# Input statistics ahead of a gating multiply, thresholds scaled on another engine, prologue and last tile in another order: one attention and expert layer on one core

## The reference

```
x = x + attention(layernorm(x))            # 16 heads of 8, one shared key and value head, causal
x = x + experts(layernorm(x))
  xn = rmsnorm(x) * gamma;  q = xn @ wq.T  # 2 halves x 8 heads x 64
  sim = q . keys                           # 2 x 8 lists of 32 per row
  best 16 of the sums sx[i] + sy[j] per head; softmax over them
  h = gelu(xn . table_down[e]) * prob;  out = sum h * table_up[e]
```

## Time and profile before

| | |
|---|---|
| median of 3 runs | 849.4 us (849.34 to 853.87) |
| the profiled execution | 852.14 us, of which the span from first to last instruction is 850.3 us |
| mean granted TensorE clock | 0.968 of full speed |
| busy, share of the span | PE 83%, PEld 58%, DVE 88%, ACT 80%, POOL 77% |
| one iteration of the loop | 47.70 us |

### The profile page before, as it was taken

How to read it: one execution, slowest core, us unless ns; L and a number is a source line. 1 busy time by engine, 2 the same in 40 slices (tenths; PEclk the granted TensorE clock), 3 DMA queues, 4 the chain that set the end, 5 groups by cost and what they waited for, 6 DMA issues and landing times.

```text
span 850.3 us, 21025 instructions
## 1 busy us (share of the span) xinstructions
PE 703.9 (83%) x6148; PEld 492.1 (58%) x6214; DVE 750.8 (88%) x2934; ACT 676.8 (80%) x927; POOL 658.2 (77%) x370
## 2 busy tenths in 40 slices
PE   3886878897979888897979888897979888887867
PEld 2652536574646656574646666574646666564746
DVE  4419599999999999999999999999999999898984
ACT  1365688989888898989888898888888898868471
POOL 2111488897979799898979799898979798887761
PEclk9897989999999999999999999999999999899988
DMA  6322121120303121120302021120302121000000
GB/s 176 57 40 56 21 55 28 29 57 10 74 2 67 19 60 26 31 55 10 74 2 67 19 60 26 35 51 10 76 0 67 19 55 27 13 21 1 20 6 7
DMA packets 34736, 32.53 MB, mean 38 GB/s; under 512 B 5520, under 2 KB 32784, under 8 KB 32976
## 3 DMA queue, kind: packets, MB, share of 16 engines
q1 hardware_dynamic: 34608, 32.12, 17.3%
q10 hardware_dynamic: 96, 0.02, 0.0%
HBM read 19.93 MB, written 5.24 MB: 30 GB/s over the span
## 4 chain that ended last, share of the span: by engine, by line
PE 47%; DVE 25%; issue 14%; ACT 9%; DMA 2%; POOL 1%; SPq 1%; DVEq 1%; ACTq 0%; POOLq 0%
DVE prob L1061 12%; PE misc L1305 6%; PE misc L1465 6%; PE score L1342 5%; PE score L1394 5%; PE score L1285 5%; PE score L1255 4%; ACT prob L750 3%; PE score L1287 3%; PE misc L1307 3%; ACT late_scores L616 2%; PE score L1258 2%; DVE halves L901 2%; DVE late_scores L907 2%; PE score L1406 2%
## 5 line engine op out<-in xcount | busy, mean ns | idle before, releaser
L516 POOL TENSOR_TENSOR acc<-acc,prob 128x1024 f32<-128x1024 f32 x184 | 435.5, 2367 | 16.2 <-POOL acc L516 0.6
L1061 DVE SCALAR_TENSOR_TENSOR prob<-score,cut,prob 128x1024 f32<-128x1024 f32 x256 | 314.5, 1277 | 22.8 <-ACT prob L750 21.4
L750 ACT ACTIVATE prob<-score,neg_lse 128x1024 f32<-128x1024 f32 x256 | 279.0, 1119 | 36.8 <-PE score L1394 30.0
L1394 PE MATMUL score<-sel_unit,pieces_t 128*128 128x512 bf16 x479 | 148.2, 395 | 72.5 <-DVE prob L1061 47.5
L643 ACT ACTIVATE probs<-score 128x512 f32<-128x512 f32 x192 | 110.2, 597 | 27.4 <-PE score L1287 23.3
L516 POOL TENSOR_TENSOR acc<-prob 128x1024 f32<-128x1024 f32 x32 | 75.6, 2361 | 64.5 <-DVE prob L1061 64.5
L1394 PEld LDWEIGHTS score<-sel_unit,pieces_t 128*128 128x128 f16 x512 | 40.1, 101 | 118.6 <-DVE prob L1061 83.4
L1342 PEld LDWEIGHTS score<-xn_kept,wdt 128*128 128x128 f32 x480 | 72.4, 191 | 29.4 <-issue 6.4
L1342 PE MATMUL score<-xn_kept,wdt 128*128 128x128 f32 x480 | 85.0, 278 | 3.8 <-DVE prob L1061 3.4
L1255 PE MATMUL score<-k_ahead,q_ahead 128*128 128x256 bf16 (+1 forms) x512 | 70.3, 246 | 12.6 <-ACT probs L643 7.0
L1465 PEld LDWEIGHTS misc<-wu,gated_t 128*128 128x128 f32 x480 | 66.0, 199 | 9.8 <-issue 1.7
(11 more groups left out here) (151 smaller groups left out, 1437.6 us busy)
## 6 DMA issues: line engine op xcount, KB each, us to landing
q_scratch<-qk_piece SPq DMA_DIRECT2D x16, 192.0 KB, 2.1
q_ahead<-q_scratch SPq DMA_DIRECT2D x16, 192.0 KB
q_stack<-q_scratch SPq DMA_DIRECT2D x16, 192.0 KB
xin<-x SPq DMA_DIRECT2D x16, 128.0 KB, 3.0
q_ahead<-q_scratch SPq DMA_DIRECT2D x16, 128.0 KB
q_stack<-q_scratch SPq DMA_DIRECT2D x16, 128.0 KB
xres<-x SPq DMA_DIRECT2D x16, 128.0 KB, 3.4
x_kept<-x SPq DMA_DIRECT2D x16, 128.0 KB, 2.0
```

The source lines that it names most:

```text
L516: eng.tensor_tensor(acc[:, j, :], so_far, prob[:, j * FH + h, :], ALU.add).then_inc(acc_added, FH - h if last else 1)
L750: eng.activation(prob[:, g, :], score[g % BUFS][:, :], ACT.Exp, bias=neg_lse[:, j, h:h + 1]).then_inc(prob_made, 1)
L1061: eng.scalar_tensor_tensor(prob[:, g, :], score[g % BUFS][:, :], cut[:, j, h:h + 1], prob[:, g, :], ALU.is_ge, ALU.mult).then_inc(prob_mas ...
L1394: ins = eng.matmul(score[g % BUFS][:, cols], pieces_t[:, j, h, :], sel_unit[:, cols], start=True, stop=True)
```

## The change

1. VectorE does `ln1(i+3)` straight after `make_y`, ahead of `gate(i-1, 0)`; it stood behind `norm_x2`.
2. `scale_cut` moves from VectorE to ScalarE, behind `xn_back`, and writes a new tensor `limit` that the masks read.
3. Prologue: the DMAs of the two expert tables (`wdt`, `wu`) go from before the first `store_pieces` to behind `stack_pieces(0)`, with a semaphore of their own. ScalarE does `xn_back(0)` ahead of `qk_middle_piece(2)`. TensorE waits for the last maxima copy of batch 1 and runs `keep_busy` twice, five matmuls each, around `xn_transpose(0)`.
4. Iteration 0: `weigh_values` and `invert_sums` come ahead of the first score maxima of batch 2.
5. Iteration 15: ScalarE does `pieces_back` ahead of `best_exp`. TensorE adds only head 2, after all pair scores; VectorE adds heads 3 to 7 with four additions.

```diff
 prologue, SyncE
-                                 (keyt[:, :], keys), (wdt[:, :], down),
-                                 (wu[:, :, :], up.rearrange("(c p) d -> p c d", p=P))):
+                                 (keyt[:, :], keys)):
                     eng.dma_start(dst, src).then_inc(weights_in, 16)
...
                 stack_pieces(0)
+                eng.dma_start(wdt[:, :], down).then_inc(tables_in, 16)
+                eng.dma_start(wu[:, :, :], up.rearrange("(c p) d -> p c d", p=P)).then_inc(tables_in, 16)
 ScalarE
+            def scale_cut(b):
+                eng.wait_ge(cut_made, every(cut_made, b))
+                if not later(b):
+                    eng.wait_ge(unit_step, 9)
+                eng.activation(limit[:, :, :], cut[:, :, :], ACT.Copy, scale=unit[:, :]).then_inc(cut_scaled, 1)
...
+                xn_back(0)
                 qk_middle_piece(2)
-                xn_back(0)
...
-                if m:
+                if m and d:
                     max_scores_back(i + 2, 0)
                 if a:
                     invert_sums(i + 1)
+                if m and not d:
+                    max_scores_back(i + 2, 0)
...
+                if f and not a:
+                    pieces_back(i, 0)
+                    pieces_back(i, 1)
                 if f:
                     best_exp(i)
...
+                if f and a:
                     pieces_back(i, 0)
                     pieces_back(i, 1)
...
                     xn_back(i + 1)
                 if f:
+                    scale_cut(i)
                     pair_probs(i, 0, 1)
 VectorE
-                eng.scalar_tensor_tensor(prob[:, g, :], score[g % BUFS][:, :], cut[:, j, h:h + 1], prob[:, g, :],
+                eng.scalar_tensor_tensor(prob[:, g, :], score[g % BUFS][:, :], limit[:, j, h:h + 1], prob[:, g, :],
...
-                eng.tensor_tensor(prob[:, 2 * FH - 2, :], ...)
-                eng.tensor_tensor(prob[:, 2 * FH - 3, :], ...)
+                for n in range(4):
+                    g = 2 * FH - 2 - n
+                    if n > 0:
+                        eng.wait_ge(late_added, n)
+                    eng.tensor_tensor(prob[:, g, :], prob[:, g, :], prob[:, g + 1, :], ALU.add).then_inc(late_added, 1)
...
                     make_y(i + 1)
+                if p:
+                    ln1(i + 3)
                 if d and f:
                     gate(i - 1, 0)
                 if f:
                     shift_best(i)
                 if a:
                     norm_x2(i + 1)
-                if p:
-                    ln1(i + 3)
...
-                if f:
-                    scale_cut(i)
 TensorE
-                eng.wait_ge(weights_in, 6 * 16)
+                eng.wait_ge(weights_in, 4 * 16)
...
                 project_qkv(2, x2_made, 0)
+                eng.wait_ge(max_kept, every(max_kept, 1))
+                keep_busy(score[1], 5)
                 xn_transpose(0, v_next_made, every(v_next_made, 2))
+                keep_busy(score[1], 5)
...
-                if m:
+                if m and d:
                     scores_for_max(i + 2, 0)
                 if a:
                     weigh_values(i + 1, 0, max_t_made, i + 1)
                     weigh_values(i + 1, 1, max_t_made, i + 1)
+                if m and not d:
+                    scores_for_max(i + 2, 0)
...
                     for h in range(4, FH):
                         pair_scores(i, 1, h, a, m)
-                        if not a and h < 7:
-                            sum_last_tile(h - 2)
...
                 if f and not a:
+                    sum_last_tile(2)
                     finish_last()
```

More of the change, by code:

```diff
@@ L162, in build @@
         cut = sb("cut", [P, TILES, FH])
+        limit = sb("limit", [P, TILES, FH])
         shifted = sb("shifted", [P, TILES, FH, TOPK])
@@ L185, in build @@
         weights_in = signal("weights_in")
+        tables_in = signal("tables_in")
         wa_in = signal("wa_in")
@@ L267, in build @@
         acc_added = signal("acc_added", TILES * (FH - 1))
-        late_added = signal("late_added", 2)
+        late_added = signal("late_added", 4)
         last_hidden = signal("last_hidden", 2)
@@ L1034, in place_cut @@
                                          ALU.mult, ALU.add).then_inc(cut_made, 1)
[L1036 to L1041, removed]
             def sum_best(b):
@@ L1066, in add_late_heads @@
                 eng.wait_ge(prob_masked, at(prob_masked, LAST, TILES * FH))
[L1067 to L1070, removed]
-                                  ALU.add).then_inc(late_added, 1)
+                for n in range(4):
[3 more added lines that the diff above has]
+                    eng.tensor_tensor(prob[:, g, :], prob[:, g, :], prob[:, g + 1, :], ALU.add).then_inc(late_added, 1)
             def gate_last(j):
@@ L1119, in prologue @@
                 eng.tensor_tensor(wkey_sq[:, :], wkey[:, :], wkey[:, :], ALU.mult).then_inc(unit_step, 1)
-                eng.wait_ge(weights_in, 6 * 16)
+                eng.wait_ge(tables_in, 2 * 16)
                 eng.tensor_scalar(wdt[:, :], wdt[:, :], gam[:, 0:1], None, ALU.mult).then_inc(setup_done, 1)
@@ L1445, in finish_last @@
                 sum_transposed(misc, acc[:, 1, :], False, False)
-                eng.wait_ge(late_added, 2)
-                sum_transposed(misc, prob[:, 2 * FH - 3, :], False, True, acc_tp)
+                eng.wait_ge(late_added, 4)
+                sum_transposed(misc, prob[:, 2 * FH - 5, :], False, True, acc_tp)
                 eng.wait_ge(x2_copied, every(x2_copied, LAST))
```

## The result

| | before | after |
|---|---|---|
| median (6 runs each) | 850.81 us (849.34 to 853.87) | 857.25 us (853.43 to 860.35) |
| profiled execution | 852.14 us, span 850.3 | 856.89 us, span 855.1 |
| mean granted TensorE clock | 0.968 | 0.964 |

The change makes the kernel slower by a little, but clear of the scatter: ratio 1.0065, 95% interval 1.0036 to 1.0095. The forecast was 843.6 us, range 836 to 853. In what follows medians are over all runs of a kernel, but the ratio of e2 leaves out its two slowest (865.5 and 866.1 us), which are in the slow state.

What follows compares the result with a forecast made beforehand. Two nearly equal loops bound it: VectorE's own list, and masks through TensorE and ScalarE back to VectorE. Terms +2.0 +0.4 -2.6 -0.5 -0.9 -3.8 -0.4 = -5.8 us gave 846.3 profiled, 843.6 median, range 836 to 853.

Steps and rivals of the forecast that it cites:

- so ln1 costs 0.96 us: Loop: moved ahead of the gate, ln1 fills the 0.55 us wait, delays the gate 0.41, of which 0.24 is absorbed.
- Late xn: Loop: beside VectorE's folds GpSimd's xn pair takes about 3.5 us instead of 1.58; 0 per iteration at full clock.
- Clock drops in the loop: Loop: TensorE's longer pause lowers its clock in 2 of 12 iterations, +1.0 us each, +2 in all (0 to +12).
- Rival 1: Loop: the clock falls in every iteration, +12 us instead of +2: 853.6 us, or 856 with second drops; chance 0.18.
- scale_cut: Move to ScalarE: nothing in iterations 0 to 13, +0.4 us in iteration 14, where the first mask must wait for ScalarE.
- Tables: Prologue: with the table DMAs moved, the first write of queries lands earlier, -2.6 us (bounds 0 and -2.6).
- keep_busy: Prologue: added matmuls let the key scores run at full clock, -0.5 us (bounds 0 and -1.7).
- Order of iteration 0: Weighted values start 1.8 us earlier, the copy of the maxima moves onto the path: -0.9 us (bounds 0 and -1.8).
- Iteration 0 itself: Iteration 0: ln1 stands where VectorE waits, so 0.
- Last tile: Iteration 15: masks end 5.0 us earlier, four additions replace two: -3.8 us (+2.5 to -5); pieces_back ahead of best_exp -0.4.
- Rival 3: Last tile or prologue gives nothing, as with additions and a half-clock sum ending the chain: 846 to 848 us; chance 0.14.

Runs made afterwards that it cites:

- e2: Kernel before with only the move of ln1 ahead of the gate: 860.66 us, ratio to before 1.0069.
- e13: Kernel after with ln1's last step made by two one-column operations instead of one of two columns, same place: 848.93 us, ratio to before 0.9959.
- e5: e3 with VectorE also waiting in the loop for both xn operations ahead of the first fold: 861.5 us, ratio to before 1.0096.
- e3: Kernel after with only ln1's last step, the addition of epsilon, moved back behind norm_x2: 848.37 us, ratio to before 0.9944.
- e4: Kernel after with scale_cut back on VectorE: 856.24 us, ratio to before 1.0042.
- e12: e9 with scale_cut back on VectorE between the folds: 843.65 us, ratio to before 0.9892.
- e1: Kernel after with ln1 back behind norm_x2, everything else of the change kept: 846.83 us, ratio to before 0.993.
- e8: e1 without the prologue's ten small matmuls and with xn copied behind the middle piece again: 845.42 us, ratio to before 0.9918.
- e9: e8 and e6 joined: ln1 back, no small prologue matmuls or earlier xn copy, heads 2 and 3 on TensorE: 844.61 us, ratio to before 0.9908.
- e10: e9 with the order of iteration 0 as in the kernel before: 843.1 us, ratio to before 0.990.
- e7: e1 with 20 small unread matmuls ahead of TensorE's last-tile wait for the four additions: 844.77 us, ratio to before 0.9905.
- e6: e1 with TensorE adding heads 2 and 3 of the last tile, VectorE making three additions: 845.13 us, ratio to before 0.9911.

## Why the prediction was wrong

The step that failed is "so ln1 costs 0.96 us", carried to the new place. The duration was read where ln1 stood before; ahead of the gate its last step is held behind GpSimd's piece of sim for 0.85 us in nearly every iteration. In the kernel before it is 18.18 us from the last mask to the next statistics; with the forecast's terms that becomes 18.18 + 0.41 - 0.24 = 18.35. e13, where the step isn't held, has 18.38; the kernel after has 19.03.

With e13 the loop takes 713.33 - 140.90 = 572.43 us. That is +0.2 against before, with 47.56 at full clock and 48.48 in two drops, where the forecast had 47.70, 48.7 and two drops. With the held step it is +7.7, and the first held step lies in the stretch of iteration 0. Over both stretches the kernel after takes 8.6 us more than e13 (630.19 against 621.60), out of the 10.6 us that forecast and measured sum lie apart. The forecast and the measured median lie 13.65 apart. Of the 3 us more, 1.4 are in the level of before (849.4 from three runs, 850.81 from six), and the rest in where the two profiled executions lie among their runs.

The sign stood in the trace of the kernel before: its `bounded` step, 128x2 too, took 0.41 us beside GpSimd's pieces in the loop and 0.17 alone, and one `ln_tmp` of the prologue 1.14.

Point by point:

- **Late xn**: right. 3.34 us (forecast 3.5), made by the folds (e5), and at full clock it takes back what the earlier fold gave (e3, e13). The forecast had read the contention in one direction only: VectorE's folds hold up GpSimd. What decided the case was a VectorE step held up by GpSimd.
- **Clock drops in the loop**: about right in this trace, three instead of two, 1.0 to 1.1 us each, and partly by luck: with the held step e2 has five and e4 six. Rival 1 named a time (853.6 to 856) close to what came, by a mechanism that did not occur: nine of twelve iterations had no drop.
- **scale_cut**: right in the loop (e12). In iteration 14 the first mask starts 5.59 us after the x2 statistics instead of 5.07: +0.5, forecast +0.4.
- **Tables**: right, 2.5 us over all traces (forecast 2.6), 1.98 in the profiled pair. In that one TensorE's new last wait is for `k_ahead` on ScalarE's queue.
- **keep_busy**: wrong in sign. The key scores did speed up, 3.42 to 1.96 us; what came earlier by it ran into the folds of batch 1. Forecast -0.5, measured +0.8 to +1.5 (e13 against e12, e1 against e8).
- **Order of iteration 0**: right, -1.0 where the clock is low in the same places (forecast -0.9); the pair e9 and e10 alone would give -1.8.
- **Iteration 0 itself** was put at 0 and took 1.33 more. 0.87 of it is the first held step of ln1, which comes ahead of the statistics that end this stretch. The rest comes before the eighth mask (19.52 instead of 19.02 us after the statistics): there too xn is late (6.08 us, before 5.58) and the clock down.
- **Last tile**: the masks were about right. The last of them ends 69.3 us after the x2 statistics of iteration 14 instead of 74.8, -5.5, where the forecast's terms for this part make -5.0. The end was mis-sized: 17.4 us from there on instead of 13.0, so +4.5, where the forecast had +1.2. The four additions took 5.71 us (forecast 5.4), the last sum 3.78 (forecast 2.0), since TensorE had waited 2.80 us and came back at half clock, and the first output matmuls 3.11 instead of 1.95 for the same reason. Rival 3 had named this. e7 shows the clock's part, and e6 that an even split between the engines avoids it.
- **Iteration 13**: -1.57 was not forecast. Its wait of 1.46 us ahead of mask 3 in the kernel before is gone after, together with the clock drop of the earlier trace rows; where the drop comes again (e9) the iteration takes 47.54 us, where not (e1) 46.76. That part is scatter of the clock.

## What to carry to other kernels

An instruction's duration belongs to its place. Least, median and most of a small step over one trace show whether it is sometimes held. Before moving one, list what the other engine that shares its SBUF ports runs at the new place, and ask both ways who holds up whom, for steps of 128x2 too. If a small step is caught, changing its form can be cheaper than moving it. Work that gets faster upstream (the key scores) or an engine that gets all of a shared task (the four additions) should be followed to what it now lies beside and who now waits.

## What the hardware showed that was not expected

- An operation on 128x2 numbers took 0.17 to 1.14 us by what GpSimd was running, and where it took over 0.25 us it ended 0.02 to 0.03 us after GpSimd's operation, in 75 of 75 cases of 16 traces; as two operations on one column each, 0.15 and 0.14 us in all 32 cases, 25 of them inside a running one (e13).
- GpSimd's own operation on 128x2, 0.73 us long, held nothing: eight `ln_tmp` steps on two columns in eight traces began with 0.2 us of it still to run and took 0.17 us.
- Holding goes both ways and in unequal parts: three short bf16 folds grew from 1.48 to 3.14 us beside GpSimd's pieces of sim, which grew only from 2.26 to 2.60; the xn pair grew from 1.58 to 3.3 to 3.5 beside the long folds, which stayed at 1.22.
- Twenty matmuls whose result nobody reads, 2.35 us, kept the clock at 1.00 and saved 1.4 us of the sum behind them (e7); ten such matmuls in the prologue, with the earlier copy of xn, made that stretch 0.8 to 1.5 us longer (e13 against e12, e1 against e8).
- TensorE's pause of 1.51 us ahead of the xn transposes stands in 11 of the 12 iterations of the loop after. The clock fell right behind it in two of them and later, among the masks, in a third; in the other eight it stayed up.
